# A three-layer block on one core: a new written-out order on all five engines, with attend visits beside score visits

## The reference, cut to what matters

```
x = x + xattn(_layernorm(x), ctx, ctx, mask)   # 32 heads of 32, 8 groups of keys/values, 257 context rows
x = x + s4(_layernorm(x), ...)                 # a long convolution over 1024 columns, plus D * u
x = x + moe(_layernorm(x), ...)                # z = x A^T (512 wide), gate = softmax of the top 16 of 64 scores,
                                               # out = (z * gate) B^T * 2
```

## Time and profile before

| | |
|---|---|
| median of 3 runs (lowest to highest) | 1304.36 us (1303.62 to 1305.89) |
| the profiled execution's own time | 1306.38 us |
| its span, first to last instruction | 1304.6 us |
| mean granted TensorE clock | 0.991 |
| busy: PE, ACT, DVE, POOL | 1243.8, 1117.4, 1057.6, 827.7 us |
| scores(2, 0) begin / scores(31, 0) begin | 116.23 / 1215.10 us of the span |

### The profile page before, as it was taken

The page is one execution under the profiler, slowest core; times in us unless marked ns, Lnnn a source line. Parts: engine busy times, 40 slices in busy tenths (PEclk is TensorE's granted clock), DMA queues, the critical chain, the costliest instruction groups (busy, mean ns, idle before and its releaser), DMA issues.

```text
span 1304.6 us, 42153 instructions
## 1 busy us (share of the span) xinstructions
PE 1243.8 (95%) x13676; PEld 1078.2 (83%) x13676; DVE 1057.6 (81%) x3560; ACT 1117.4 (86%) x3329; POOL 827.7 (63%) x1259
## 2 busy tenths in 40 slices
PE   2579999999999999999999999999999999999997
PEld 2457888888888888888888888888888888888876
DVE  6988888888888887888888888887888888888753
ACT  3689989989999998999999898988999898998841
POOL 5437667666666776666677666667766666776420
PEclk9979999999999999999999999999999999999999
DMA  8544454454455455445545454454545445554210
GB/s 211 138 121 121 136 150 121 128 145 130 124 133 140 121 136 137 134 125 131 137 120 146 127 148 117 125 137 128 141 125 145 125 121 141 127 142 120 61 59 33
DMA packets 270940, 166.45 MB, mean 128 GB/s; under 512 B 195433, under 2 KB 253298, under 8 KB 270722
## 3 DMA queue, kind: packets, MB, share of 16 engines
q1 hardware_dynamic: 270722, 163.74, 46.7%
HBM read 128.50 MB, written 34.08 MB: 125 GB/s over the span
## 4 chain that ended last, share of the span: by engine, by line
PE 85%; DVE 4%; SPq 3%; ACT 2%; issue 2%; DMA 2%; POOL 1%; DVEq 0%; POOLq 0%; ACTq 0%
PE ps_p L565 25%; PE ps_p L651 15%; PE ps_p L636 15%; PE ps_p L664 14%; PE ps_p L597 9%; PE ps_s L577 8%; SPq L384 2%; ACT pr L832 1%; DVE ms L1395 1%; DMA dn<-den 1%; DMA turn<-lasts 1%; DVE x L1250 0%; POOL lastp L1095 0%; ACT pts L784 0%; SPq L431 0%
## 5 line engine op out<-in xcount | busy, mean ns | idle before, releaser
L832 ACT ACTIVATE pr<-ms,negmax 128x256 f32<-128x256 f32 x1024 | 513.9, 504 | 12.0 <-DVE negmax L1395 11.9
L1395 DVE CUSTOM_DVE_ANT_0 ms<-ps_s,neg_mask,last 128x256 f32<-128x256 f32 x1024 | 456.6, 470 | 35.4 <-PE ps_s L577 29.9
L784 ACT ACTIVATE pts<-ps_p 128x512 f32<-128x512 f32 x512 | 295.9, 592 | 48.3 <-PE ps_p L565 44.2
L565 PE MATMUL ps_p<-ident,pr 128*128 128x128 f32 x2048 | 306.2, 278 | 9.4 <-DVE wa_lo L1195 4.5
L565 PEld LDWEIGHTS ps_p<-ident,pr 128*128 128x128 f32 x2048 | 240.1, 141 | 44.7 <-issue 16.7
L832 ACT ACTIVATION_READ_ACCUMULATOR pr<-ms,negmax 128x1 f32 x1024 | 199.8, 195 | 0.0
L1053 POOL TENSOR_TENSOR kt<-kr,kt 128x512 fp32r<-128x512 f32 x128 | 165.1, 1290 | 28.4 <-ACT kt L784 27.9
L651 PE MATMUL ps_p<-wa_hi,ut_hi 128*128 128x288 f32 x512 | 177.6, 347 | 1.6 <-DVE ut_lo L1195 1.6
L651 PE MATMUL ps_p<-wa_lo,ut_hi 128*128 128x288 f32 x512 | 151.2, 295 | 0.0
L651 PE MATMUL ps_p<-wa_hi,ut_lo 128*128 128x288 f32 x512 | 150.6, 294 | 0.0
L1095 POOL TENSOR_TENSOR lastp<-lastp 128x256 f32<-128x256 f32 (+4 forms) x320 | 129.7, 405 | 22.7
(11 more groups left out here) (140 smaller groups left out, 2717.3 us busy)
## 6 DMA issues: line engine op xcount, KB each, us to landing
kx<-in_ctx SPq DMA_DIRECT2D x512, 64.0 KB, 2.4
cx<-in_ctx SPq DMA_DIRECT2D x128, 256.0 KB, 3.1
xq<-in_x SPq DMA_DIRECT2D x32, 512.0 KB, 4.3
turn_q<-xq SPq DMA_DIRECT2D x32, 512.0 KB, 3.8
qx<-turn_q SPq DMA_DIRECT2D x128, 128.0 KB, 2.9
xr<-in_x SPq DMA_DIRECT2D x32, 512.0 KB, 4.3
out_x<-tmp SPq DMA_DIRECT2D x32, 512.0 KB, 5.2
dn<-den SPq DMA_DIRECT2D x512, 2.0 KB, 2.2
```

The source lines that it names most:

```text
L565: mm = pe.transpose(into[:, j * P:(j + 1) * P], source, ident[:, :])
L784: return act.activation(out, in_, ACT.Copy, scale=scale)
L832: act.activation(pr[:, b % 2, g, :], ms[:, n % MS, :], ACT.Exp, bias=negmax[:, n % MS:n % MS + 1], scale=-1.0, accum_out=den[:, b, g:g + 1 ...
L1395: dve.tensor_tensor_reduce(ms[:, n % MS, :], ps_s[:, g % GPH, g // GPH * SW:(g // GPH + 1) * SW], neg_mask[:, 0:SW], 1.0, last[:, it % 2, ...
```

## The change: what it does

It alters no instruction and no function outside the `iteration` functions, the lists of head and tail, and `BANKS`. All five engines get a new order. On PE, in an iteration:

- three attend visits stand directly beside a score visit: attend 4, 5 before scores 1; attend 0, 1 after scores 2; attend 2, 3 at the end, before scores 0 of the next iteration. The fourth (attend 6, 7) has one `pair_chunk` between it and scores 1.
- transposes stand in longer rows: five groups before scores 2 (`pair_chunk` 3, out 1, `pair_chunk` 4, gated, `pair_chunk` 5) and four before attend 2, 3 (`pair_chunk` 11, z 0, `pair_chunk` 12, z 1). Chunks 11 and 12 of a tile move from the next iteration into its own.
- `convolve` k=0 stands before scores 3, and both halves of the convolution use bank 3; out chunks 0 and 1 no longer follow each other.

The line numbers of `after` are one higher than before on PE and 11 lower on ACT, POOL and DVE.

The diff, cut to `BANKS`, the whole of PE's iteration, and the places of ACT and DVE that the prediction speaks of (SP and POOL are reordered in the same manner):

```diff
 BANKS = {
-    "pair": (1, 0, 0, 1, 0, 2, 0, 3, 1, 0, 0, 1, 0, 3, 1, 0,),
-    "out": (0, 1,),
+    "pair": (0, 1, 1, 3, 2, 3, 2, 1, 2, 1, 1, 0, 2, 1, 0, 3,),
+    "out": (3, 1,),
     "u": (3, 1,),
-    "z": (0, 3,),
-    "g": (1,),
-    "y": (2, 1,),
-    "f": (3, 2,),
-    "b": (1, 2,),
-    "o": (3, 2, 1, 1,),
-    "keys": (1,),
-    "router": (2,),
-    "sums": (2,),
-    "dft": (1,),
-    "rows": (0,),
-    "strip": (1, 3, 0,),
-    "w": (1, 0, 1, 3, 2, 1, 0, 2, 3, 2, 2, 3, 0, 2, 2, 2,),
+    "z": (1, 0,),
+    "g": (0,),
+    "y": (3, 3,),
+    "f": (0, 2,),
+    "b": (1, 0,),
+    "o": (2, 3, 3, 3,),
+    "keys": (3,),
+    "router": (0,),
+    "sums": (3,),
+    "dft": (0,),
+    "rows": (1,),
+    "strip": (2, 0, 0,),
+    "w": (3, 1, 3, 1, 2, 0, 0, 1, 3, 0, 3, 0, 3, 2, 3, 0,),
 }
...
             def iteration(it, odd):
                 scores(it, 0)
                 if on(it - 1):
-                    pair_chunk(it - 1, 11)
-                    pair_chunk(it - 1, 12)
-                if on(it - 2):
-                    experts(it - 2, 1, 0, 1)
-                if on(it - 1):
                     pair_chunk(it - 1, 13)
-                if on(it - 2):
-                    experts(it - 2, 1, 1, 3)
-                if on(it - 1):
                     pair_chunk(it - 1, 14)
                 if on(it - 2):
-                    experts(it - 2, 1, 3, 4)
+                    experts(it - 2, 1, 0, 2)
                 if on(it - 1):
                     pair_chunk(it - 1, 15)
                 if on(it - 2):
-                    experts(it - 2, 1, 4, 6)
+                    experts(it - 2, 1, 2, 8)
                 if on(it - 1):
                     attend(it - 1, 4); attend(it - 1, 5)
-                if on(it - 2):
-                    experts(it - 2, 1, 6, 8)
                 scores(it, 1)
-                if on(it - 2):
-                    experts(it - 2, 0, 0, 1)
                 pair_chunk(it, 0)
+                if on(it - 1):
+                    attend(it - 1, 6); attend(it - 1, 7)
                 pair_chunk(it, 1)
                 if on(it - 2):
-                    experts(it - 2, 0, 1, 3)
-                if on(it - 1):
-                    attend(it - 1, 6); attend(it - 1, 7)
+                    experts(it - 2, 0, 0, 4)
+                if on(it - 1):
+                    out_chunk(it - 1, 0)
+                if on(it - 2):
+                    experts(it - 2, 0, 4, 5)
                 pair_chunk(it, 2)
                 if on(it - 2):
-                    experts(it - 2, 0, 3, 5)
+                    experts(it - 2, 0, 5, 8)
                 pair_chunk(it, 3)
-                if on(it - 2):
-                    experts(it - 2, 0, 5, 6)
-                if on(it - 1):
-                    out_chunk(it - 1, 0)
+                if on(it - 1):
                     out_chunk(it - 1, 1)
-                if on(it - 2):
-                    experts(it - 2, 0, 6, 8)
                 pair_chunk(it, 4)
-                scores(it, 2)
                 if on(it - 2):
                     gated_chunk(it - 2)
                 pair_chunk(it, 5)
+                scores(it, 2)
                 attend(it, 0); attend(it, 1)
+                if on(it - 2):
+                    expand(it - 2, 0, 0, 4)
+                    expand(it - 2, 1, 0, 1)
                 pair_chunk(it, 6)
                 if on(it - 2):
-                    expand(it - 2, 0, 0, 4)
+                    expand(it - 2, 1, 1, 2)
                 pair_chunk(it, 7)
-                if on(it - 2):
-                    expand(it - 2, 1, 0, 2)
+                if on(it - 1):
+                    u_chunk(it - 1, 0)
                 pair_chunk(it, 8)
                 if on(it - 2):
-                    expand(it - 2, 1, 2, 3)
-                if on(it - 1):
-                    u_chunk(it - 1, 0)
-                if on(it - 2):
-                    expand(it - 2, 1, 3, 4)
+                    expand(it - 2, 1, 2, 4)
                 if on(it - 1):
                     u_chunk(it - 1, 1)
+                    convolve(it - 1, 0, 0, 4)
                 scores(it, 3)
                 pair_chunk(it, 9)
                 if on(it - 1):
-                    convolve(it - 1, 0, 0, 4)
-                    convolve(it - 1, 1, 0, 1)
+                    convolve(it - 1, 1, 0, 2)
                 pair_chunk(it, 10)
                 if on(it - 1):
-                    convolve(it - 1, 1, 1, 8)
+                    convolve(it - 1, 1, 2, 8)
+                pair_chunk(it, 11)
+                if on(it - 1):
                     z_chunk(it - 1, 0, 1 - odd)
+                pair_chunk(it, 12)
+                if on(it - 1):
+                    z_chunk(it - 1, 1, 1 - odd)
                 attend(it, 2); attend(it, 3)
-                if on(it - 1):
-                    z_chunk(it - 1, 1, 1 - odd)
...
                 exp(it, 25)
+                last_exp(it, 2)
+                pair_copy(it, 10)
                 exp(it, 26)
+                if on(it + 1):
+                    k_high(it + 1, 2)
+                    q_high(it + 1, 1)
                 exp(it, 27)
-                pair_copy(it, 10)
                 exp(it, 28)
-                if on(it + 1):
-                    q_high(it + 1, 1)
+                pair_copy(it, 11)
                 exp(it, 29)
-                if on(it + 1):
-                    k_high(it + 1, 2)
                 if on(it - 1):
                     z_high(it - 1, 0)
                 exp(it, 30)
-                last_exp(it, 2)
                 if on(it - 1):
                     z_high(it - 1, 1)
                 exp(it, 31)
                 output(it, 1)
-                pair_copy(it, 11)
                 last_exp(it, 3)
...
                 maximum(it, 5)
                 maximum(it, 6)
+                if on(it - 2):
+                    route_step(it - 2, 0)
                 maximum(it, 7)
+                if on(it - 2):
+                    route_step(it - 2, 1)
                 if on(it - 1):
                     normalisers(it - 1)
                 if on(it - 2):
-                    route_step(it - 2, 0)
+                    route_step(it - 2, 2)
                 maximum(it, 8)
...
                 maximum(it, 23)
-                if on(it + 1):
-                    q_turn(it + 1, 0)
-                if on(it - 2):
-                    third_residual(it - 2, 1, odd)
-                if on(it - 1):
-                    u_low(it - 1, 0)
+                if on(it - 1):
+                    u_low(it - 1, 1)
+                    second_residual(it - 1, 0, 1 - odd)
                 maximum(it, 24)
                 maximum(it, 25)
-                if on(it - 1):
-                    u_low(it - 1, 1)
+                if on(it + 1):
+                    k_turn(it + 1, 2)
                 maximum(it, 26)
+                if on(it - 1):
+                    z_stats(it - 1, 0, 1 - odd)
                 maximum(it, 27)
-                if on(it - 1):
-                    second_residual(it - 1, 0, 1 - odd)
                 maximum(it, 28)
```

More of the change, by code:

```diff
@@ L760, in _ @@
+            attend(1, 0); attend(1, 1); pair_chunk(1, 5); pair_chunk(1, 6); pair_chunk(1, 7); u_chunk(0, 0)
+            scores(1, 3); u_chunk(0, 1); pair_chunk(1, 8); convolve(0, 0, 0, 4); weight_chunk(7, 1)
+            pair_chunk(1, 9); convolve(0, 1, 0, 2); pair_chunk(1, 10); convolve(0, 1, 2, 4); pair_chunk(1, 11)
+            convolve(0, 1, 4, 8); pair_chunk(1, 12); z_chunk(0, 0, 0); attend(1, 2); attend(1, 3); z_chunk(0, 1, 0)
             for it in range(HEAD, TAIL):
                 iteration(it, odd=it % 2)
-            pair_chunk(30, 11); pair_chunk(30, 12); scores(31, 0); experts(29, 1, 0, 1); pair_chunk(30, 13)
@@ L778, in _ @@
-            experts(31, 0, 0, 8); gated_chunk(31); expand(31, 0, 0, 4); expand(31, 1, 0, 4)
+            scores(31, 0); pair_chunk(30, 13); pair_chunk(30, 14); pair_chunk(30, 15); experts(29, 1, 0, 8)
+            attend(30, 4); attend(30, 5); scores(31, 1); pair_chunk(31, 0); pair_chunk(31, 1)
+            attend(30, 6); attend(30, 7); experts(29, 0, 0, 2); pair_chunk(31, 2); out_chunk(30, 0)
+            experts(29, 0, 2, 8); pair_chunk(31, 3); out_chunk(30, 1); pair_chunk(31, 4); gated_chunk(29)
@@ new lines, in _ @@
+            scores(31, 2); pair_chunk(31, 5); attend(31, 0); attend(31, 1); expand(29, 0, 0, 4); expand(29, 1, 0, 1)
+            pair_chunk(31, 6); expand(29, 1, 1, 2); u_chunk(30, 0); pair_chunk(31, 7); expand(29, 1, 2, 4)
+            u_chunk(30, 1); convolve(30, 0, 0, 1); pair_chunk(31, 8); convolve(30, 0, 1, 4); pair_chunk(31, 9)
+            scores(31, 3); convolve(30, 1, 0, 2); pair_chunk(31, 10); convolve(30, 1, 2, 4); z_chunk(30, 0, 0)
+            convolve(30, 1, 4, 7); pair_chunk(31, 11); convolve(30, 1, 7, 8); pair_chunk(31, 12); z_chunk(30, 1, 0)
@@ new lines, in _ @@
+            attend(31, 2); attend(31, 3); pair_chunk(31, 13); pair_chunk(31, 14); pair_chunk(31, 15)
```

(16 more changed lines are left out.)

438 lines of the change are left out of this document (204 added, 234 removed).

## The result

The change is slower: 1362.61 us (1360.96 to 1366.46) against 1303.99 (1303.56 to 1305.89), a ratio of 1.0451 with a 95% interval of 1.0431 to 1.047. The profiled execution has a span of 1359.2 us. The forecast was 1293.

A forecast was written before the change was run, and what follows sets the result against it. TensorE's own stream was taken as the bound. Per iteration 0.47 + 0.13 - 0.20 = 0.40 us, by 29 = 11.6, off the profiled 1306.38 gives 1294.8; the run median, 2.0 lower, gives 1293 us, range 1284 to 1304.

The forecast's parts named there:

- Visits: On PE, 8 gaps between visits become 5, with direct attend-to-scores passages at no extra cost: 0.47 us saved an iteration.
- rival 2: On PE, each change of tile shape costs the same 0.08 us, so three fewer save 0.23: 1300 us; chance 0.12.
- Out chunks: On PE, out chunks stand apart in banks 3 and 1, with nothing fresh waited for: 0.13 us saved an iteration.
- (a): z chunk 1 takes bank 0 from pair chunk 11 and waits for its copy: 0 to 0.1 us.
- New waits: Two new PE waits for ACT's copies in each iteration, together 0.2 us lost, bounds 0 and 0.6.
- (b): experts k=1 takes bank 2 and waits for the late copy of pair chunk 12: about 0.1 to 0.3 us.
- rival 1: The two new waits vanish as ACT runs ahead: 0.60 us saved an iteration, so 1287 us; chance 0.17.
- SP's queue and POOL's have room: their moved DMAs cost 0: In the iteration, SP's moved DMAs and POOL's moved products are hidden by loads an iteration ahead: cost 0.
- The cover that I named: A tile's loads are an iteration ahead, hiding moved DMAs; without it, a scores visit would wait for keys.
- Rival 4: Convolution halves share bank 3, so k=1 waits for second_residual 0; one us late gives 1313 us; chance 0.10.
- rival 6: Shuffled loads and set-up make the head lose 12 us and more, giving 1305 to 1310 us; chance 0.04.
- rival 5: Twenty transposes in a row before scores 2 let PE's clock fall to 1.2 GHz: 19 us, 1312; chance 0.04.

The follow-up runs named there:

- hybrid: The change on all engines, but SP's iteration order as before (SP's head and tail as in the change, five calls moved at the seams): 1289.03 us.
- residual mid: Against the change: SP's load_residual(it) moved ahead of move_den(it, 0) instead of directly ahead of load_x(it + 2): 1316.64 us.

## Why the prediction was wrong

- *Visits, 0.47 us an iteration: right.* The gap that was put back costs 0.22 for my 0.19, and the direct passage has no price. So rival 2, an equal price for each change of tile shape, is refuted here: what counts by these rows is how often PE leaves the visits for other work. The Trainium skill says that changing the tiling mode drains TensorE ("TensorEngine Tiling (Array Packing)", Key Properties). No run here refutes the drain itself; what fails is the drain taken as the whole price in equal shares, 0.08 where 0.22 was measured.
- *Out chunks, 0.13: right together with the visits.* No run parts the two. With no waits I had 0.60 us saved in an iteration; the shortest period is 0.53 shorter, and wait (a) takes the other 0.07. *New waits (a) and (b), 0.20: mis-sized.* (a) is 0.07: z chunk 1's transposes begin 0.18 us behind the last one of chunk 12, where the others follow each other by 0.11, and 0.14 us behind the end of ACT's copy of chunk 11. (b) isn't there. In the hybrid and in the change, 12's copy ends 3.90 us after 11's copy begins, not 4.15, and PE reaches `experts` after 4.07, as laid out. This comes near rival 1, which has a period of 37.1, with 37.20 measured.
- *"SP's queue and POOL's have room: their moved DMAs cost 0": the step that failed.* I costed SP's queue by how much there is in it, not by who waits at its end. The wait for it stood in the trace of before, where DVE lost 47.2 us to `dn<-den` with little cost to PE (DVE's waits: total, times, longest):

```profile
DVE dn L1457 <- DMA dn<-den: 47.2, 27, 3.8
```

  Idle time of DVE that costs nothing was the margin, and the change used it up: deadline 1.7 us sooner (7.4 instead of 9.1 us after scores 0), data 1.7 us later (9.5 instead of 7.8). That wait is the 54.6 us, and the slower pace behind it most of a further 11.7. None of my rivals was this mechanism. The cover that I named, loads that are an iteration ahead, is not there for `dn<-den` and `last<-turn`: their data are made in the kernel shortly before and needed shortly behind. Rival 4 (both halves in bank 3) took 0.9 us in all in the change, in one wait outside the 29 iterations, and rival 6 (the head) 2.4.
- *The clock (rival 5): wrong cause.* Twenty transposes in a row take 2.27 us and keep the clock at 1.00 in the iterations of all versions without such waits. It fell behind long waits of PE: in iteration 24, after the 3.12 us idle, the window 1006.64 to 1009.51 has 0.50, that is 1.2 GHz, with an `experts` matmul each 0.24 us instead of 0.13. In 12 iterations `experts` k=0 began 2.3 us or more late, from start to start. Of these, 7 show such a stretch, and none of the other 17 does. Each of the 7 lost 1.3 to 1.6 us more by it, 10.8 us together, most of the 11.7.

## What to carry to other kernels

When a change moves many queues, follow each queue to the instruction behind its last item and compare arrival with deadline, in the changed order on both sides; an average share of a queue doesn't show this. A harmless wait in the profile of before ("DVE waits for a DMA, PE doesn't care") is a margin with a size, and it should be written down as one. And when a step has several customers, as the normalisers had, look at all of them before moving the step; here only bringing its data earlier helped.

## What the runs showed of the hardware beyond that

A 16 KB store needed 5.2 us to land (the median in the change; 3.3 in the kernel before) when two 512 KB loads and one set of keys were issued directly ahead of it. With three other calls between those two loads (residual mid), at the same number of issues, it needed 3.5. Where the granted clock fell to 1.2 GHz behind a late start of 2.3 us or more, that cost 1.3 to 1.6 us more (10.8 us over 7 iterations).
